# Second attention: the copy of the finished output groups moved from ScalarE to VectorE, at the head of the next step

## The chip, the core and the metric

The kernel runs on one core of a Trainium2 chip. The metric is the device time of one execution in microseconds (us). The engines are TensorE (PE in the rows; PEld is its weight load), ScalarE (ACT), VectorE (DVE), GpSimd (POOL) and SyncE (SP, which here only issues DMAs). Each engine works through its own instructions in order and waits for others on semaphores.

## The reference

Four layers follow one another on 16 sequences of 256 tokens with 128 features. Each is `x = x + layer(layernorm(x))`: a first attention with two heads, a feed-forward network, a second attention, and the same network again. The change lies in the second attention (16 heads of 8 features, causal):

```
qkv = encodings @ attn_w.T + attn_b
qkv = qkv.reshape(b, n, HEADS, 3 * HEAD).transpose(0, 2, 1, 3)
q, k, v = jnp.split(qkv, 3, axis=-1)
scores = jnp.einsum('bhki,bhqi->bhkq', k, q) / math.sqrt(HEAD)
scores = jnp.where(mask, scores, NEG_INF)
probs = jax.nn.softmax(scores, axis=2)
combined = jnp.einsum('bhkq,bhkl->bhql', probs, v)
out = combined.transpose(0, 2, 1, 3).reshape(b, n, HIDDEN)
return out @ out_w.T + out_b
```

## The kernel before, in words

The tokens are cut into 8 blocks of 512 (two sequences each), called 0 to 7 here. In the second attention a block takes 8 steps: 4 groups of 4 heads, times 2 sequences. Step `n` works on group `n // 2`, sequence `n % 2`. The loop is software-pipelined: while block `b` gets its exponentials and its output, block `b+1` gets its maxima, and block `b+2` its normalised input and its q and k.

On TensorE one step consists, in this order, of `pe_second` for the first head pair (the scores of block `b`, into two PSUM banks), `pe_first` (the scores of block `b+1`, from which only the row maxima are wanted; each has a last matmul with the mask), `pe_second` for the second pair, and `pe_values` of the step before (the probabilities times the values, into `o_bank`). Behind that, some steps carry one more piece: step 0 the transposes of the maxima, step 1 the transposes of the normalised input, steps 2 and 3 the q and the k product, step 4 the v product, step 5 more transposes of maxima, step 6 the output projection of block `b-1`.

ScalarE takes the exponential of each `pe_second` (`act_exp`, `b_prob`), copies the maxima (`act_max`, `b_negative_max`), the q and k products (`act_hi`) and the transposed input. GpSimd masks each exponential (`pool_mask`) and multiplies the output with the inverse denominators (`pool_normalise`). VectorE reduces each `pe_first` to maxima (`dve_first`, two instructions that write `b_segment_max`), and computes the layer norm: `bn_stats` and `bn_aggr` at the head of step 0, and `dve_apply` (`xn`) at the end of step 0. It also makes the low parts of q and k (`dve_lo`, heads of steps 3 and 4), adds the bias to v (`dve_v`, step 5) and adds the projected output to `X` (`dve_down`, step 7). The order on every engine is written out by hand in `pe_step`, `act_body`, `dve_body` and `pool_body`.

`o_bank` is one PSUM bank. It collects a group over two steps, is copied to `b_o`, and is free for the next group only then: the first `pe_values` of a group waits for `b_output_copied` (`s_oc`). When the fourth group of a block is copied, in the block that follows, SyncE stores `b_o` to DRAM (L1772), and when that has landed loads it back in another layout as `b_oT` (L1776) and its denominators as `b_den` (L1777). VectorE takes their reciprocal (`dve_inverse`, at the end of step 2), and SyncE stores and loads that too. The reciprocal stands in VectorE's queue ahead of the low part of q and of the maxima of step 3.

In block 7 no maxima remain to be made. TensorE, ScalarE and VectorE already work on the gate of the next network there: after steps 2, 4 and 6 TensorE makes a gate product, ScalarE its tanh, and VectorE four instructions on it (`f_gate`, `f_hidden`, `f_h_hi`, `f_h_lo`).

Of the kernel before, what the change touches and what calls it, by code (L numbers as in the profile page):

```python
# [26 lines left out]
SEQS = 2  # L27
# [16 lines left out]
GROUPS = 4  # L44
# [41 lines left out]
def build(nc, io):  # L86
    ctx = ExitStack()
    with ctx:
# [1102 lines left out]
        def attention_b(link):  # L1191
# [18 lines left out]
            o_sb = sb("b_o", [P, GROUPS, TOK])  # L1210
# [11 lines left out]
            o_bank = banks3[:, 2, :]  # L1222
# [259 lines left out]
            def act_out(act, b, g):  # L1482
                act.wait_ge(s_pv, STEPS * b.t + SEQS * (g + 1))
                if g == 0:
                    wait(act, s_os, 16 * b.t)
                nc.scalar.activation(o_sb[:, g, :], o_bank[:, :], ACT.Copy).then_inc(s_oc, 1)
# [13 lines left out]
            def act_body(act, b, before, one, two):  # L1500
                prev, nxt = link["prev"], link["next"]
                n1, n2 = b.after(1), b.after(2)
                for n in range(STEPS):
                    act_exp(act, b, n, 0)
                    if n == MAX1_AT + 1:
                        act_max_rows(act, b, 1)
                    if one and n == MAX0_AT + 1:
                        act_max_rows(act, n1, 0)
                    act_exp(act, b, n, 1)
                    if is_block(b, 0) and n == 0:  # L1510
                        prev["act_tail"](act)
                    if n and n % SEQS == 0:
                        act_out(act, b, n // SEQS - 1)
                    if before and n == 0:
                        act_out(act, b.after(-1), GROUPS - 1)
                    if n == MAX1_AT:
                        act_max(act, b, 1)
                    if two and n == T_AT:
                        act_xT(act, n2)
                    if two and n == Q_AT:  # L1520
                        act_hi(act, n2, 0)
                    if two and n == K_AT:
                        act_hi(act, n2, 1)
                    if one and n == MAX0_AT:
                        act_max(act, n1, 0)
                    if not one and n == T_AT:
                        act.wait_ge(s_pv, STEPS * LAST)
                        nxt["act_xhi"](act, FIRST_BLOCK)
                    if not one and n in GATE_AT:
                        nxt["act_tanh"](act, FIRST_BLOCK, GATE_AT[n], HEAD_PAIR)  # L1530
                if not one:
                    act_out(act, b, GROUPS - 1)
                    nxt["act_tanh"](act, FIRST_BLOCK, KC - 1, HEAD_PAIR)
                    nxt["act_xhi"](act, SECOND_BLOCK)
# [40 lines left out]
            def dve_max(dve, m, half):  # L1575
# [5 lines left out]
                nc.vector.tensor_tensor(mx[half][:, :, 1, :, :].rearrange("p s j g -> p g s j"),  # L1581
                                        part[:, :, :, :, 1], part[:, :, :, :, 2], ALU.max).then_inc(s_mx, 1)

            def dve_inverse(dve, b):

                dve.wait_ge(s_ol, 32 * (b.t + 1))
                nc.vector.reciprocal(den_inv[:, :], den[:, :]).then_inc(s_inv, 1)
# [6 lines left out]
            def dve_body(dve, b, before, one, two):  # L1594
# [3 lines left out]
                for n in range(STEPS):  # L1598
                    if two and n == 0:
                        norm.dve_stats(dve, n2)  # L1600
                    if two and n == Q_AT + 1:
                        dve_lo(dve, n2, 0)
                    if two and n == K_AT + 1:
                        dve_lo(dve, n2, 1)
                    if one and n == V_AT + 1:
                        dve_v(dve, n1)
                    if one and before and n == OUT_AT + 1:
                        dve_down(dve, b.after(-1))
                    if one:
                        dve_first(dve, n1, n)  # L1610
                    if is_block(b, 0) and n == 0:
                        prev["dve_down"](dve, LAST_BLOCK)
                    if two and n == T_AT - 1:
                        norm.dve_apply(dve, n2, False)
                    if one and n == MAX0_AT - 1:
                        dve_max(dve, n1, 0)
                    if one and not two and n == OUT_AT:
                        nxt["norm"].dve_stats(dve, FIRST_BLOCK)
                    if one and not two and n == STEPS - 1:
                        norm.dve_free(dve)  # L1620
                        nxt["norm"].dve_apply(dve, FIRST_BLOCK, True)
                    if not one and n == T_AT:
                        nxt["dve_xlo"](dve, FIRST_BLOCK)
                        nxt["norm"].dve_stats(dve, SECOND_BLOCK)
                    if not one and n in GATE_AT:
                        nxt["dve_gate"](dve, FIRST_BLOCK, GATE_AT[n], HEAD_PAIR)
                        nxt["dve_hlo"](dve, FIRST_BLOCK, GATE_AT[n])
                    if before and n == INVERSE_AT:
                        dve_inverse(dve, b.after(-1))
# [323 lines left out]
```

## Time and profile before

| | |
|---|---|
| median of 3 runs | 743.64 us (742.78 to 744.47) |
| the profiled execution | 742.03 us, span 740.2 us |
| busy: PE, DVE, ACT, POOL | 671.3, 493.8, 453.2, 431.1 us of the span |
| chain that ended last | PE 52%, DVE 15%, issue 10%, POOL 8%, ACT 8%, DMA 6% |
| copies of output groups on ScalarE | 32, first at 342.2 us, last at 553.3 us |

Times of rows count from the start of the span. The profiled execution, 742.03 us, stands 1.6 us under the median of the three runs. In a timeline row stand the start, the time from the start of the first of the grouped instructions to the end of the last, the engine, the line, the operation with output and inputs, the count, and in brackets how long the engine was idle before and what ended that.

### The profile page before, as it was taken

To read this page: it belongs to the slowest core of one execution; us is meant where nothing else is said; L and a number is where in the kernel's file an instruction comes from. 1 tells how busy PE (TensorE), PEld (TensorE's weight loads), DVE (VectorE), ACT (ScalarE), POOL (GpSimd) and SP (SyncE) were. 2 spreads that over 40 slices of the span, in tenths; PEclk is the share of its full clock that TensorE was granted. 3 is DMA by queue.
4 is the path that set the end of the run, shared out by engine and by line. 5 is a ranking of instruction groups with operands and counts; after the bars stand their busy time and mean duration, and the time that the engine had idled before them with its cause. 6 is when DMAs were issued, how large, how long until landed. Compare 5 with 4: busy or idle time off the path is not lost.

```text
span 740.2 us, 13952 instructions
## 1 busy us (share of the span) xinstructions
PE 671.3 (91%) x4706; PEld 470.9 (64%) x4706; DVE 493.8 (67%) x958; ACT 453.2 (61%) x801; POOL 431.1 (58%) x443
## 2 busy tenths in 40 slices
PE   3889997899999989998999999998788899999997
PEld 1455655577877766665555555555446677877785
DVE  6779997657765686466777777675658457766521
ACT  2678886465666655546666666665655465666664
POOL 4545552477787776443444554544555687787773
PEclk9999999899999999999999999999969999999999
DMA  6111320000000004432556565563112000000001
GB/s 188 39 26 35 62 30 2 0 1 0 1 0 0 1 1 138 148 115 76 201 183 205 193 206 184 190 206 103 63 35 84 0 15 14 0 14 15 15 14 29
DMA packets 33028, 52.47 MB, mean 71 GB/s; under 512 B 4560, under 2 KB 9680, under 8 KB 32976
## 3 DMA queue, kind: packets, MB, share of 16 engines
q1 hardware_dynamic: 32784, 51.53, 22.2%
q8 instruction: 30, 0.49, 0.3%
q10 hardware_dynamic: 192, 0.26, 0.1%
q14 instruction: 22, 0.18, 0.1%
HBM read 27.15 MB, written 24.38 MB: 70 GB/s over the span
## 4 chain that ended last, share of the span: by engine, by line
PE 52%; DVE 15%; issue 10%; POOL 8%; ACT 8%; DMA 6%; SPq 1%; DVEq 0%; ACTq 0%; POOLq 0%
PE banks L220 49%; ACT b_prob L1478 3%; DVE b_segment_max L1571 3%; DMA b_o_dram<-b_o 3%; POOL f_h_lo L1149 3%; POOL f_g_lo L1156 2%; DVE xn L182 2%; DVE a_mx L652 2%; ACT a_prob L553 1%; DMA b_den<-b_o_dram 1%; DVE a_prob L666 1%; PE banks L212 1%; ACT f_g_hi L1044 1%; POOL b_prob L1681 1%; DVE a_straight L637 1%
## 5 line engine op out<-in xcount | busy, mean ns | idle before, releaser
L1156 POOL TENSOR_TENSOR f_g_lo<-f_gelu,f_g_hi 128x512 fp32r<-128x512 f32 x127 | 167.2, 1325 | 62.4 <-ACT f_g_hi L1044 61.9
L1043 ACT ACTIVATE f_gelu<-banks,cols 128x512 f32<-128x512 f32 x128 | 88.4, 691 | 134.4 <-PE banks L220 111.6
L1681 POOL TENSOR_SCALAR_AFFINE_SELECT b_prob<-b_prob 128x512 f32<-128x512 f32 x128 | 82.2, 644 | 108.0 <-ACT b_prob L1478 107.7
L1571 DVE TENSOR_REDUCE b_segment_max<-banks 128x6 f32<-128x768 f32 x128 | 116.2, 949 | 34.2 <-PE banks L220 34.2
L1478 ACT ACTIVATE b_prob<-banks 128x768 f32<-128x768 f32 x128 | 102.4, 807 | 55.9 <-PE banks L220 55.9
L220 PE MATMUL banks<-f_g_hi,whi 128*128 128x512 f32 x320 | 130.3, 407 | 2.3 <-POOL f_g_lo L1156 1.8
L220 PE MATMUL banks<-f_g_lo,whi 128*128 128x512 f32 x320 | 126.6, 396 | 0.0
L1149 POOL TENSOR_TENSOR f_h_lo<-f_hidden,f_h_hi 128x512 fp32r<-128x512 f32 x60 | 77.5, 1292 | 58.6 <-DVE f_h_hi L1095 58.6
L220 PE MATMUL banks<-f_h_hi,whi 128*128 128x512 f32 x256 | 106.0, 414 | 3.9 <-POOL f_h_lo L1149 2.3
L220 PE MATMUL banks<-f_h_lo,whi 128*128 128x512 f32 x256 | 102.3, 400 | 0.0
L1044 ACT ACTIVATE f_g_hi<-banks,cols 128x512 fp32r<-128x512 f32 x128 | 87.5, 683 | 0.0
L1088 DVE SCALAR_TENSOR_TENSOR f_gate<-f_tanh,banks 128x512 f32<-128x512 f32 x64 | 43.4, 678 | 62.5 <-ACT f_tanh L1035 62.5
L220 PE MATMUL banks<-f_xn_split,whi 128*128 128x512 f32 x256 | 74.1, 414 | 0.7 <-DVE f_hidden L1092 0.6
L182 DVE TENSOR_SCALAR xn<-X,mv,rstd 128x128 f32<-128x128 f32 (+1 forms) x104 | 72.2, 760 | 0.5 <-POOL rstd L207 0.4
L220 PEld LDWEIGHTS banks<-f_g_hi,whi 128*128 128x128 f32 x320 | 60.3, 188 | 17.7 <-POOL f_g_lo L1156 3.6
L220 PEld LDWEIGHTS banks<-f_g_lo,whi 128*128 128x128 f32 x320 | 60.3, 188 | 13.1 <-issue 0.2
L220 PEld LDWEIGHTS banks<-f_h_hi,f_h_lo 32*128 32x128 f32 x512 | 37.2, 187 | 46.4 <-ACT b_prob L1478 23.5
L220 PE MATMUL banks<-f_h_hi,f_h_lo 32*128 32x256 f32 (+1 forms) x512 | 55.2, 304 | 10.9 <-ACT b_prob L1478 7.5
L220 PE MATMUL banks<-b_prob,b_values 128*16 128x256 f32 (+1 forms) x1024 | 57.2, 343 | 6.9 <-POOL b_prob L1681 5.5
L220 PEld LDWEIGHTS banks<-f_h_hi,whi 128*128 128x128 f32 x256 | 48.9, 191 | 22.1 <-ACT f_g_hi L1044 3.9
L220 PEld LDWEIGHTS banks<-f_xn_split,whi 128*128 128x128 f32 x256 | 49.7, 197 | 15.0 <-issue 1.8
L220 PEld LDWEIGHTS banks<-f_h_lo,whi 128*128 128x128 f32 x256 | 48.8, 191 | 11.4 <-issue 0.7
(125 smaller groups left out, 1051.4 us busy)
## 6 DMA issues: line engine op xcount, KB each, us to landing
f_h_hi<-b_q_dram SPq DMA_DIRECT2D x16, 512.0 KB, 4.2
f_h_lo<-b_k_dram SPq DMA_DIRECT2D x16, 512.0 KB, 5.1
b_o_dram<-b_o SPq DMA_DIRECT2D x8, 1024.0 KB, 4.3
b_q_dram<-b_q_hi SPq DMA_DIRECT2D x16, 256.0 KB, 3.4
b_k_dram<-b_k_hi SPq DMA_DIRECT2D x16, 256.0 KB, 3.7
w_stage<-in_wF SPq DMA_DIRECT2D x8, 352.0 KB, 3.4
b_q_dram<-b_q_lo SPq DMA_DIRECT2D x8, 256.0 KB, 3.5
b_k_dram<-b_k_lo SPq DMA_DIRECT2D x8, 256.0 KB, 3.5
```

The source lines that it names most:

```text
L182: nc.vector.tensor_scalar(xn[:, s, :], X[:, bass.ds(TILES * t + s, 1), :], mv[:, s, 0:1], rstd[:, s:s + 1], ALU.subtract, ALU.mult).then_i ...
L212: last = nc.tensor.transpose(bank[:, s * P:(s + 1) * P], xn[:, s, :], ident[:, :])
L220: return nc.tensor.matmul(out, lhsT, rhs, start=start, stop=stop)
L652: nc.vector.reduce_max(mx[s][:, :, :], score[:, :, :].rearrange("p h (q k) -> p h q k", q=2), AX.X).then_inc(s_mx, 1)
L1043: nc.scalar.activation(gf[c % 2][:, :], z_bank[c % 2], ACT.Gelu, scale=scale).then_inc(s_gf, 1)
L1044: nc.scalar.activation(hi[:, c, :], z_bank[c % 2], ACT.Gelu, scale=scale).then_inc(s_ghi[c % 2], 1)
L1088: nc.vector.scalar_tensor_tensor(out=uu[slot][:, :], in0=th[slot][:, :], scalar=1.0, in1=a[:, :], op0=ALU.add, op1=ALU.mult).then_inc(s_u, 1)
L1149: nc.gpsimd.tensor_tensor(hlo[n.odd][:, c, :], hf[c % 2][:, :], hhi[n.odd][:, c, :].bitcast(F32), ALU.subtract).then_inc(s_hlo[c % 2], 1)
L1156: nc.gpsimd.tensor_tensor(lo[:, c, :], gf[c % 2][:, :], hi[:, c, :].bitcast(F32), ALU.subtract).then_inc(s_glo[c % 2], 1)
L1478: nc.scalar.activation(prob[n % 2][:, p, :, :, :], second_banks(b, p)[:, :, 0:3 * P].rearrange("p b (c q) -> p c b q", c=3), ACT.Exp, scal ...
L1571: nc.vector.reduce_max(seg[:, g, s, 2 * p:2 * p + 2, :], first_pass[:, 2 * p:2 * p + 2, 0:3 * P].rearrange("p b (c k) -> p b c k", c=3), A ...
L1681: nc.gpsimd.affine_select(out=pr, in_=pr, compare_op=ALU.is_ge, fill=0.0, base=0, pattern=[[0, 4], [1, P]], channel_multiplier=-1).then_in ...
```

## The change

The function `dve_out` copies a finished group on VectorE. It is called ahead of the maxima (`dve_first`) in steps 3, 5 and 7 for groups 0, 1 and 2, and in step 1 of the next block for group 3. The calls of `act_out` in ScalarE's steps are gone; on ScalarE it stood behind the second exponential of steps 2, 4 and 6 and of step 0 of the next block. ScalarE keeps one copy: group 3 of block 7, behind its last step. `dve_out` waits for the same semaphores as `act_out` and counts the same one up.

```
--- before
+++ after
@@ act_body
                     act_exp(act, b, n, 1)
                     if is_block(b, 0) and n == 0:
                         prev["act_tail"](act)
-                    if n and n % SEQS == 0:
-                        act_out(act, b, n // SEQS - 1)
-                    if before and n == 0:
-                        act_out(act, b.after(-1), GROUPS - 1)
                     if n == MAX1_AT:
                         act_max(act, b, 1)
@@
+            def dve_out(dve, b, g):
+                dve.wait_ge(s_pv, STEPS * b.t + SEQS * (g + 1))
+                if g == 0:
+                    wait(dve, s_os, 16 * b.t)
+                nc.vector.tensor_copy(o_sb[:, g, :], o_bank[:, :]).then_inc(s_oc, 1)
+
@@ dve_body
                     if one and before and n == OUT_AT + 1:
                         dve_down(dve, b.after(-1))
+                    if before and n == 1:
+                        dve_out(dve, b.after(-1), GROUPS - 1)
+                    if n > 1 and n % SEQS:
+                        dve_out(dve, b, n // SEQS - 1)
                     if one:
                         dve_first(dve, n1, n)
```

VectorE's queue before, from the end of step 0 to the start of step 3 of a block in the middle (the reductions into `b_segment_max` are those of steps 0 to 3, in pairs):

```order
L1571 TENSOR_REDUCE b_segment_max<-banks 128x6
L182 TENSOR_SCALAR xn<-X,mv,rstd 128x128 [waits b_xn_transposed,b_ln_rstd]
L182 TENSOR_SCALAR xn<-X,mv,rstd 128x128 x3
L1571 TENSOR_REDUCE b_segment_max<-banks 128x6 [waits b_first_scores]
L1571 TENSOR_REDUCE b_segment_max<-banks 128x6
L1571 TENSOR_REDUCE b_segment_max<-banks 128x6 [waits b_first_scores]
L1571 TENSOR_REDUCE b_segment_max<-banks 128x6
L1587 RECIPROCAL b_den_inv<-b_den 128x64 [waits b_output_loaded]
L1557 SCALAR_TENSOR_TENSOR b_q_lo<-banks,cols,b_q_hi 128x512 [waits b_hi_ready]
L1571 TENSOR_REDUCE b_segment_max<-banks 128x6 [waits b_first_scores]
L1571 TENSOR_REDUCE b_segment_max<-banks 128x6
```

The same stretch of VectorE's queue after the change:

```order
L1567 TENSOR_REDUCE b_segment_max<-banks 128x6
L182 TENSOR_SCALAR xn<-X,mv,rstd 128x128 [waits b_xn_transposed,b_ln_rstd]
L182 TENSOR_SCALAR xn<-X,mv,rstd 128x128 x3
L1584 COPY b_o<-banks 128x512 [waits b_values_weighted]
L1567 TENSOR_REDUCE b_segment_max<-banks 128x6 [waits b_first_scores]
L1567 TENSOR_REDUCE b_segment_max<-banks 128x6
L1567 TENSOR_REDUCE b_segment_max<-banks 128x6 [waits b_first_scores]
L1567 TENSOR_REDUCE b_segment_max<-banks 128x6
L1589 RECIPROCAL b_den_inv<-b_den 128x64 [waits b_output_loaded]
L1553 SCALAR_TENSOR_TENSOR b_q_lo<-banks,cols,b_q_hi 128x512 [waits b_hi_ready]
L1584 COPY b_o<-banks 128x512 [waits b_output_stored,b_values_weighted]
L1567 TENSOR_REDUCE b_segment_max<-banks 128x6 [waits b_first_scores]
```

The first copy (group 3 of the block before) now stands behind the reduction and the `xn` of step 0; the second (group 0 of this block) behind the reciprocal and the low part of q.

VectorE's queue in block 7, at the end of the third gate's four instructions (`-` before, `+` after; `xn` and `X` belong to the input of the next network and to the output of block 6):

```order
 L1099 TENSOR_TENSOR f_h_lo<-f_hidden,f_h_hi 128x512 [waits f2_hidden_hi]
+L1584 COPY b_o<-banks 128x512 [waits b_values_weighted]
 L182 TENSOR_SCALAR xn<-X,mv,rstd 128x128 [waits f2_xn_transposed,f2_ln_rstd]
 L182 TENSOR_SCALAR xn<-X,mv,rstd 128x128 x3
-L1592 TENSOR_TENSOR X<-banks,X 128x512 [waits b_bias_added_to_x,b_projected]
+L1594 TENSOR_TENSOR X<-banks,X 128x512 [waits b_bias_added_to_x,b_projected]
```

Here the copy of group 2 stands behind the four instructions on the third gate; the copies of groups 0 and 1 stand in the same way behind the first gate and the reciprocal, and behind the second gate.

## Rows read from the trace of the kernel before

**Rows 1.** Waits, 335 to 555 us: who waited for whom, in total, times, longest
```profile
DVE b_den_inv L1587 <- DMA b_den<-b_o_dram: 10.7, 6, 2.6
```

**Rows 2.** Groups of instructions, 335 to 555 us: busy us, mean ns of one
```profile
L1486 ACT ACTIVATE b_o<-banks 128x512 f32<-128x512 f32 x32 | 19.1, 597 | 7.6 <-PE banks L220 5.6 <-DMA b_o_dram<-b_o 2.0
...
L1563 DVE TENSOR_TENSOR b_values<-banks,rows 128x512 f32<-128x512 f32 x7 | 4.8, 692 | 1.6 <-PE banks L220 0.8
L1557 DVE SCALAR_TENSOR_TENSOR b_k_lo<-banks,cols,b_k_hi 128x512 fp32r<-128x512 f32 x6 | 4.5, 751 | 4.3 <-ACT b_k_hi L1470 4.3
...
L1557 DVE SCALAR_TENSOR_TENSOR b_q_lo<-banks,cols,b_q_hi 128x512 fp32r<-128x512 f32 x6 | 4.0, 668 | 1.1 <-ACT b_q_hi L1470 1.1
...
L1095 DVE CAST f_h_hi<-f_hidden 128x512 fp32r<-128x512 f32 x3 | 1.3, 427 | 0.1
```

**Rows 3.** Chain of work that ended last, 440 to 470 us: start, us, what
```profile
444.15 0.83 DVE b_segment_max L1571
445.02 1.22 DVE xn L182 x4
...
446.66 1.82 DVE b_segment_max L1571 x2
448.48 0.04 issue
448.52 3.21 PE banks L220 x34
```

**Rows 4.** Timeline of block 4, end of step 0 to step 4, and step 7
```profile
444.08 0.60 ACT L1486 ACTIVATE b_o<-banks 128x512 f32<-128x512 f32 x1
...
444.58 0.59 ACT L1492 ACTIVATE b_negative_max<-banks 8x512 fp32r<-8x512 f32 x1
...
446.44 0.84 PE L220 MATMUL banks<-b_prob,b_values 128*16 128x256 f32 x16
...
451.75 0.69 ACT L1470 ACTIVATE b_q_hi<-banks,cols 128x512 fp32r<-128x512 f32 x1 [0.43 <-PE banks L220]
...
452.71 0.55 DVE L1587 RECIPROCAL b_den_inv<-b_den 128x64 f32<-128x64 f32 x1 [1.34 <-DMA b_den<-b_o_dram]
...
453.20 0.45 PE L220 MATMUL banks<-f_h_hi,f_h_lo 32*128 32x256 f32 x4 [0.34 <-ACT b_prob L1478]
...
453.58 0.84 PE L220 MATMUL banks<-b_prob,b_values 128*16 128x256 f32 x16
...
453.75 1.81 DVE L1571 TENSOR_REDUCE b_segment_max<-banks 128x6 f32<-128x768 f32 x2
...
455.62 0.39 PE L220 MATMUL banks<-f_h_lo,f_h_hi 32*128 32x256 f32 x2
...
467.23 1.82 DVE L1571 TENSOR_REDUCE b_segment_max<-banks 128x6 f32<-128x768 f32 x2 [0.33 <-PE banks L220]
```

**Rows 5.** Timeline of block 6, step 0 and step 4
```profile
497.98 1.82 DVE L1571 TENSOR_REDUCE b_segment_max<-banks 128x6 f32<-128x768 f32 x2 [0.69 <-PE banks L220]
...
499.16 0.60 ACT L1486 ACTIVATE b_o<-banks 128x512 f32<-128x512 f32 x1
...
510.46 0.65 PE L220 MATMUL banks<-f_h_lo,f_h_hi 32*128 32x256 f32 x8 [1.97 <-DVE b_segment_max L1571]
```

**Rows 6.** Timeline of block 7, `pe_values` of steps 2, 4 and 6 and VectorE beside it
```profile
535.57 0.84 PE L220 MATMUL banks<-b_prob,b_values 128*16 128x256 f32 x16 [1.40 <-ACT b_o L1486]
...
538.93 0.54 DVE L1587 RECIPROCAL b_den_inv<-b_den 128x64 f32<-128x64 f32 x1
...
542.57 1.48 PE L220 MATMUL banks<-b_prob,b_values 128*16 128x256 f32 x16
...
544.73 1.00 DVE L1099 TENSOR_TENSOR f_h_lo<-f_hidden,f_h_hi 128x512 fp32r<-128x512 f32 x1
...
551.74 1.48 PE L220 MATMUL banks<-b_prob,b_values 128*16 128x256 f32 x16 [2.08 <-POOL b_prob L1681]
```

**Rows 7.** Timeline: TensorE's first work after two other gaps
```profile
43.05 1.33 PE L449 MATMUL banks<-ident,a_prob 128*128 128x128 f32 x5 [2.74 <-ACT a_prob L568]
...
276.92 0.63 PE L212 MATMUL banks<-ident,xn 128*128 128x128 f32 x4 [2.26 <-DVE xn L182]
```

**Rows 8.** TensorE in three stretches: stretch, us, busy (count), granted clock, DMA share, GB/s
```profile
44.00:46.00 2.00, 2.00 (x7) 0.50 0.29 107
277.00:280.00 3.00, 3.00 (x16) 1.00 0.00 0
510.50:513.50 3.00, 3.00 (x28) 0.51 0.28 87
```

## Prediction

> **What bounds the kernel now.** I read the shares and the chain of the page first, then the waits of the stretch of the second attention (335 to 555 us), then the chain of waits and the timeline of one block in the middle, block 4, and last the two blocks that differ, 6 and 7. On the page TensorE is busy 91% and ends most of the chain; that would say that a copy on any other engine is free. The chain inside block 4 says otherwise [rows 3]: from the reduction of step 0 over `xn` to the reduction of step 1 it runs on VectorE, back to back, and TensorE's next first scores start 0.04 us after the reduction ends. So VectorE has no room just where two of the four copies will stand. The second thing to see is the wait for the denominators [rows 1]: six times VectorE stands until `b_den` has landed, 10.7 us in all. In block 4 it stands 1.34 us [rows 4]. Behind the reciprocal wait the low part of q and the reduction of step 3, which starts at 453.75 and, 1.81 us long, ends at 455.56; TensorE's first scores of step 4 start at 455.62. That wait is thus already at the edge of the path. Whatever makes the denominators later is paid by TensorE one for one.
>
> **What is taken away.** ScalarE loses 31 copies of 0.60 us [rows 2]. What does it gain on the path? In step 0 the copy of group 3 ends as `b_negative_max` starts (444.58), but that waits for TensorE's transposes, so it could start hardly earlier. In step 2 ScalarE stands idle for 0.43 us before `b_q_hi` until the q product is there, the copy being long over [rows 4]. Steps 4 and 6 have the v product and the output projection on TensorE in the same place. I value the removal at 0. The upper bound of the gain stands with the rivals.
>
> **What one copy costs on VectorE.** The trace has no VectorE copy from PSUM. Nearest are three-input and two-input passes over the same 128x512 from PSUM: 668, 692 and 751 ns; from below, the cast from SBUF at 427 ns [rows 2]. I take 0.66 us, by the nearest rows, and keep 0.43 and 0.75 as ends. Instructions that follow one another start about 0.08 us before the end of the one ahead: `b_den_inv` starts at 452.71, and after its 0.55 and the 0.67 of `b_q_lo` the reduction starts at 453.75 and not at 453.93, two overlaps in 1.04 us [rows 2, 4]. So a copy pushes what stands behind it by 0.58 and is itself complete after 0.66.
>
> The cast's 427 ns is a rate for data in SBUF. The Trainium skill (VectorE: DVE Perf Modes, "Why PSUM operands drop a tier") says that fp32 from PSUM gets no fast mode, and its table of cycles (same page, "The TRN2 errata") would give 120 + 512 cycles at 0.96 GHz, an estimate of 0.658 us. By it the lower end falls away; the sum is the same.
>
> **A block in the middle (1 to 5), step by step, on block 4's times.**
> - Step 7 of the block before: the copy of group 2 stands ahead of the reduction, before which VectorE was idle 0.33 us [rows 4]. It delays it by 0.58 - 0.33 = 0.25. The reduction, the maxima, statistics and `xn` behind it are back to back, so 0.25 arrives at step 1.
> - Step 1: the copy of group 3 starts where the reduction started, 446.66 + 0.25 = 446.91, and ends at 447.57. ScalarE had it done at 444.68. The output group is copied 2.9 us later. `pe_values` of step 0 (446.44) writes the same bank and must wait until 447.6: TensorE and all behind it, the transposes of the normalised input too, go back by 1.15 us.
> - The store, its landing, the load of the denominators: SyncE issues them one after another from the copy on, and nothing in them gets shorter. The reciprocal moves from 452.71 to 455.6.
> - Step 3: reciprocal and low part of q take 1.04, so the copy of group 0 starts at 456.65 and ends at 457.3. `pe_values` of step 2, which follows the second scores (453.20) and started at 453.58, now waits for that copy: 457.35, which is 3.75 later. The reduction starts at 457.23, ends at 459.05, and TensorE, with the k product still to do, reaches the first scores of step 4 at 455.62 + 3.75 = 459.4. The 1.15 of step 1 is contained in this 3.75, since the later wait swallows the earlier.
> - The copy of group 1 in step 5 stands behind the bias of v with some idle time around it: 0.2 at most, which the wait for the exponentials covers. Were that cover gone it would be 0.58.
> - SyncE's later queue (the q and k rows for block b+2) goes back with the block, not more: their deadlines shift by as much.
>
> Per block 3.75, five blocks: 18.8. Of this, copies of 0.43 us would take off three times 0.23, or 0.7 per block, and copies of 0.75 add 0.3.
>
> **Block 6.** No `xn` stands between. The reduction of step 0 starts at 497.98 [rows 5], plus 0.25, plus 1.82 less 0.08: the copy starts at 499.97 and ends at 500.63, where ScalarE's ended at 499.76. Denominators 0.9 later, the copy of group 0 adds 0.58, and the first scores of step 4, already waiting 1.97 for the reduction, come 1.5 later. Block 0 has three copies and no denominators: 0.3.
>
> **Block 7.** Nothing delays group 3, but groups 0 to 2 stand behind the gates. Step 3: the reciprocal at 538.93 is behind the first gate and cannot start much earlier, since the denominators are no sooner there; the copy follows at 539.4 and is done at 540.0. `pe_values`, at 535.57, comes 4.4 later. As ScalarE is free during that time, exponentials are ahead afterwards; I count 2.7 as staying. Step 5: `f_h_lo` ends at 545.73, the copy 0.58 later at 546.3, `pe_values` was at 542.57: 3.7. Step 7 is the same again, 4.0, less the 2.08 that TensorE waited for masks before the next `pe_values` [rows 6]: 1.9. Together 8.3.
>
> **The clock.** In the middle blocks TensorE will stand from the end of the second scores (453.20 + 0.45 + 1.15 = 454.8) to 457.35, a gap of 2.55 us. After the gap of 1.97 us that ended at 510.46 the granted clock was 0.51 (the 1.2 GHz level) for the 3 us from 510.5; after 2.74 us (43.05) it was 0.50; after 2.26 us (276.92) it stayed at 1.00 [rows 5, 7, 8]. In three microseconds at half clock TensorE, which is what bounds after the gap (values, k product, second scores), loses 1.5 us. I take the fall in every middle block: 5 x 1.5 = 7.5. Its bounds are 0 and, with one more low stretch per block, 15.
>
> The Trainium skill (TensorE: Matmul & The Clock Gate, "HAM oscillation — how this bites in real kernels") describes a loop with a wait in each turn that puts the clock back each time, at a price of half the throttled time. By that rule the fall recurs in every block; the row after 276.92 shows that a gap near this length need not do it.
>
> **The sum.** 18.8 + 1.5 + 0.3 + 8.3 = 28.9, with the clock 36.4. The profiled execution took 742.0, so 778.4; the median of the runs stood 1.6 higher: 780.
>
> **The rivals.**
> - The same waits, but the clock stays up: 743.6 + 28.9 = 772.5. For it speaks the one gap of 2.26 us without a fall, against it the other two.
> - The denominators' path is absorbed. If stores and loads run quicker once they are not beside the row loads, or if the first copy finds its place earlier, only the direct waits count: 1.15 in five blocks, and block 7: 5.8 + 0.3 + 8.3 = 14.4 on the median, 758, or somewhat less. Against it: the wait for `b_den` is in six of seven blocks already.
> - Not slower: ScalarE's exponentials are what holds TensorE in many steps (the second scores at 453.20 waited 0.34 for them), and with 31 copies gone the exponentials start earlier. If that pays 0.5 in each copy's step it is -15.5; if only where the negative maxima follow a copy, 7 x 0.5 = -3.5, and 740. It decides if VectorE's copies fall into its idle time, that is if step 1's reduction is not on the chain. The chain says it is [rows 3].
> - More than forecast: two low-clock stretches per block, or the late low part of q holds SyncE's queue so that the q and k rows come too late: 790 and above.
>
> **Chances.** Forecast 0.51 (own range 770 to 788), clock stays 0.24 (768 to 776), absorbed 0.13 (750 to 764), more 0.06, not slower 0.06, half of it within 0.2%. The range that holds eight in ten is 760 to 788. A measurement here tells about 0.2%, 1.5 us, from no change. Slower 0.94, same 0.03, faster 0.03.
>
> **What would show it.** In the profile after: `b_o` on VectorE near 0.66 us; in a middle block the copy of group 3 directly behind `xn`; `pe_values` of step 0 released by the copy with 1.1 us of wait; about 3 us of idle time before the reciprocal where it was 1.34, and `pe_values` of step 2 released by the copy of group 0 after 2.5 us; middle blocks 3.5 to 5.5 us longer each; a granted clock near 0.5 behind that gap in blocks 1 to 5. I am wrong if the middle blocks grow by less than 2 us, if the reciprocal does not move, or if ScalarE's exponentials release TensorE earlier in steps 2, 4 and 6.

## The result and the profile after

| | before | after |
|---|---|---|
| median | 744.06 us (742.78 to 749.5) | 785.07 us (783.79 to 787.98, 4 runs) |
| profiled execution | 742.03 us, span 740.2 us | 787.98 us, span 786.1 us |
| busy: PE, DVE, ACT, POOL | 671.3, 493.8, 453.2, 431.1 us | 689.4, 510.6, 436.3, 430.9 us |
| granted clock, mean | 0.976 | 0.944 |

The change made the kernel slower by 5.4% (ratio 1.0542, interval 1.0481 to 1.0603). Forecast were 780 us, so the forecast fell short by 5. Of the page after, lines of its parts 1, 2 and 4: busy time with share and instructions, the granted clock in 40 slices, the chain that ended last.

```profile
PE 689.4 (88%) x4706; PEld 479.5 (61%) x4706; DVE 510.6 (65%) x989; ACT 436.3 (56%) x770; POOL 430.9 (55%) x443
...
PEclk9999999999999999999898898998878989999999
...
PE 52%; DVE 19%; issue 9%; POOL 6%; DMA 6%; ACT 6%; DVEq 1%; SPq 0%; ACTq 0%; POOLq 0%
```

ScalarE is rid of 17 us and VectorE has 17 us more, neither of them near its limit. The span grew by 45.9. PE's busy time rose too, though it has no instruction more: the same matmuls at a lower clock.

The waits of the second attention after (335 to 602 us): in total, times, longest.

```profile
PE banks L220 <- DVE b_o L1584: 33.3, 13, 4.5
DVE b_den_inv L1589 <- DMA b_den<-b_o_dram: 22.0, 6, 4.7
```

The first line did not exist before; the second was 10.7 us for the same six waits [rows 1]. They are two ends of one thing: VectorE stands for the denominators, and TensorE stands for the copy that is queued behind them.

Block 4 after, timeline from the end of step 0 to step 4, VectorE, SyncE and the releases on TensorE:

```profile
468.97 1.69 DVE L182 TENSOR_SCALAR xn<-X,mv,rstd 128x128 f32 x4
470.58 0.68 DVE L1584 COPY b_o<-banks 128x512 f32<-128x512 f32 x1
...
471.29 0.36 SPq L1778 DMA_DIRECT2D b_o_dram<-b_o  x1
471.31 0.84 PE L220 MATMUL banks<-b_prob,b_values 128*16 128x256 f32 x16 [0.84 <-DVE b_o L1584]
...
477.88 0.44 PE L220 MATMUL banks<-f_h_hi,f_h_lo 32*128 32x256 f32 x4 [0.34 <-ACT b_prob L1478]
...
479.35 0.55 DVE L1589 RECIPROCAL b_den_inv<-b_den 128x64 f32<-128x64 f32 x1 [3.46 <-DMA b_den<-b_o_dram]
479.82 0.65 DVE L1553 SCALAR_TENSOR_TENSOR b_q_lo<-banks,cols,b_q_hi 128x512 fp32r<-128x512 f32 x1
480.39 0.68 DVE L1584 COPY b_o<-banks 128x512 f32<-128x512 f32 x1
...
481.13 1.48 PE L220 MATMUL banks<-b_prob,b_values 128*16 128x256 f32 x16 [2.81 <-DVE b_o L1584]
```

Read it downwards as one chain: `xn`, the copy of group 3 right behind it, SyncE's store 0.03 us after the copy's end, the reciprocal 8.1 us behind the store, the low part of q, the copy of group 0, and TensorE, which had stood 2.81 us. Against [rows 4] the reciprocal's idle time has grown from 1.34 to 3.46 us. The last row shows something else: the 16 matmuls take 1.48 us where they took 0.84. TensorE by stretches of the same block (us, busy and count, granted clock, DMA share, GB/s):

```profile
475.00:479.00 4.00, 2.98 (x34) 1.00 0.28 74
479.00:480.00 1.00, 0.00 (x0) 0.81 0.00 0
480.00:481.00 1.00, 0.00 (x0) 0.50 0.15 33
481.00:486.00 5.00, 4.87 (x33) 0.50 0.63 192
486.00:487.00 1.00, 1.00 (x11) 0.78 0.24 90
```

The clock fell to its lower level (1.2 GHz) while TensorE stood, at about 479.6, and came back at about 486.4. In blocks 1 to 5 it fell each time in this gap, which was 3.61, 3.21, 2.51, 2.81 and 2.86 us long; in block 6 it fell 0.5 us after TensorE had resumed. The same view of blocks 1 to 5 after, one row each, and of all five before:

```profile
363.10:397.50 34.40, 27.32 (x324) 0.90 0.47 159
397.50:430.80 33.30, 27.68 (x324) 0.90 0.49 161
430.80:465.80 35.00, 29.66 (x324) 0.85 0.47 152
465.80:498.80 33.00, 27.80 (x320) 0.90 0.49 163
498.80:530.90 32.10, 27.03 (x322) 0.95 0.51 168
```

```profile
359.80:496.80 137.00, 126.83 (x1600) 1.00 0.59 196
```

**Where the 45.9 us of span are.** I measure a block from the first copy into `b_max` at its head to the next block's. The heads of blocks 1, 6 and 7, before, then after:

```profile
359.75 0.18 DVE L1579 COPY b_max<-b_segment_max 128x16 f32<-128x16 f32 x1
...
496.84 0.37 DVE L1579 COPY b_max<-b_segment_max 128x16 f32<-128x16 f32 x1
...
527.47 0.17 DVE L1579 COPY b_max<-b_segment_max 128x16 f32<-128x16 f32 x1
```

```profile
363.11 0.18 DVE L1575 COPY b_max<-b_segment_max 128x16 f32<-128x16 f32 x1
...
530.88 0.31 DVE L1575 COPY b_max<-b_segment_max 128x16 f32<-128x16 f32 x1
...
564.25 0.16 DVE L1575 COPY b_max<-b_segment_max 128x16 f32<-128x16 f32 x1
```

Blocks 1 to 5 took 137.1 us and take 167.8: +30.7. Block 6 took 30.6 and takes 33.4: +2.7. Ahead of block 1 there are 3.4 us. Block 0's head comes 1.4 later, behind code that the change doesn't touch: the clock fell at 278.2 behind a gap of 2.27 us, and behind the same gap it had stayed up before [rows 7, 8]. In block 0 a stretch at the lower clock, 332.8 to 336.3, costs about 1.6, as its matmuls of 128x512 take 0.63 us and not 0.40. The execution of the profile was also the slowest of the four, 2.9 us over their median. Block 7, from its head to the second `pe_values` of step 7, took 24.3 us and takes 33.0: +8.7. Its rows:

```profile
574.80 0.54 DVE L1589 RECIPROCAL b_den_inv<-b_den 128x64 f32<-128x64 f32 x1
575.26 0.62 DVE L1584 COPY b_o<-banks 128x512 f32<-128x512 f32 x1
576.03 1.48 PE L220 MATMUL banks<-b_prob,b_values 128*16 128x256 f32 x16 [4.50 <-DVE b_o L1584]
...
586.03 1.48 PE L220 MATMUL banks<-b_prob,b_values 128*16 128x256 f32 x16 [3.87 <-DVE b_o L1584]
...
596.03 2.76 PE L220 MATMUL banks<-b_prob,b_values 128*16 128x256 f32 x32 [3.84 <-DVE b_o L1584]
```

From block 7's head these three are at 11.8, 21.8 and 31.8 us; they were at 8.1, 15.1 [rows 6] and 21.4. The second half of the last row, from 597.26, is what stood at 551.74. TensorE also had its lower clock for about 18.6 us of this stretch where before it had it for 10.2; what that costs beside the waits is not separated here. The sum, 30.7 + 2.7 + 3.4 + 8.7, is 45.5; the other 0.4 of the 45.9 lie behind block 7's last `pe_values`.

### The profile page after: what moved, and what is told of

It reads as the page before. It is cut to its first block, busy times and chain, and to the rows that moved or that the text cites. A ratio compares the mean times of both kernels' runs of the same rounds, so it can differ in the third digit from the quotient of the medians.

```text
span 786.1 us, 13950 instructions
## 1 busy us (share of the span) xinstructions
PE 689.4 (88%) x4706; PEld 479.5 (61%) x4706; DVE 510.6 (65%) x989; ACT 436.3 (56%) x770; POOL 430.9 (55%) x443
## 4 chain that ended last, share of the span: by engine, by line
PE 52%; DVE 19%; issue 9%; POOL 6%; DMA 6%; ACT 6%; DVEq 1%; SPq 0%; ACTq 0%; POOLq 0%
PE banks L220 49%; DMA b_o_dram<-b_o 4%; DVE b_segment_max L1567 3%; DVE xn L182 3%; POOL f_h_lo L1149 2%; DMA b_den<-b_o_dram 2%; ACT b_prob L1478 2%; POOL f_g_lo L1156 2%; DVE a_mx L652 2%; DVE b_o L1584 2%; ACT a_prob L553 1%; DVE f_hidden L1092 1%; PE banks L212 1%; DVE a_prob L666 1%; DVE stats L171 1%
## 5 line engine op out<-in xcount | busy, mean ns | idle before, releaser
L220 PE MATMUL banks<-b_prob,b_values 128*16 128x256 f32 (+1 forms) x1024 | 62.9, 371 | 36.0 <-DVE b_o L1584 33.3
L220 PE MATMUL banks<-f_xn_split,whi 128*128 128x512 f32 x256 | 75.7, 421 | 1.3 <-DVE f_hidden L1092 1.0
L220 PEld LDWEIGHTS banks<-f_g_lo,whi 128*128 128x128 f32 x320 | 60.9, 190 | 13.4 <-issue 0.2
L220 PE MATMUL banks<-f_h_hi,f_h_lo 32*128 32x256 f32 (+1 forms) x512 | 56.4, 318 | 10.4 <-ACT b_prob L1478 7.6
L220 PEld LDWEIGHTS banks<-b_prob,b_values 128*16 128x16 f32 x1024 | 25.8, 103 | 59.0 <-issue 27.4
```

The source lines that it names most:

```text
L220: return nc.tensor.matmul(out, lhsT, rhs, start=start, stop=stop)
```

## The experiments

The theory: the time goes to the place of the copies, not to their engine. Group 3's copy behind `xn` makes the denominators late, and that holds the copy of group 0 and with it TensorE; block 7 pays apart; the clock falls behind the gaps. Rivals: the copies' own time on VectorE, ScalarE's share in the path, or the clock as the real cause.

### Group 3 back on ScalarE

```
+ if before and n == 0: act_out(act, b.after(-1), GROUPS - 1)   # in act_body
- if before and n == 1: dve_out(dve, b.after(-1), GROUPS - 1)   # in dve_body
```

> The changed kernel, with the copy of group 3 (block b-1) given back to ScalarE in step 0; groups 0 to 2 stay on VectorE. Theory (position: the time is lost because the copy of group 3 stands behind the reduction and xn of step 0, which makes the denominators and with them step 3 late): the denominators come as before, a middle block keeps only the copy of group 0 behind the low part of q, 0.8 us, no gap of TensorE over 2 us and so no fall of the clock there; block 7 keeps its 8 to 9 us. Sum 5 x 0.8 + 0.8 + 0.4 + 8.9 = 14, about 758 us. Rival (load: VectorE simply has 31 copies of 0.6 us more to do, wherever they stand): seven copies fewer of 31 give back a fourth to a fifth of the 41 us, about 776 us.

Measured: 763.09 us (759.73 to 764.39), ratio 1.0251 (1.0186 to 1.0317): without this one copy 22 us of the 41 are gone, 5 fewer than expected. `b_den_inv` waits 9.4 us in all, where it was 10.7 before the change. Block 3:

```profile
430.04 0.55 DVE L1591 RECIPROCAL b_den_inv<-b_den 128x64 f32<-128x64 f32 x1 [1.22 <-DMA b_den<-b_o_dram]
431.08 0.68 DVE L1586 COPY b_o<-banks 128x512 f32<-128x512 f32 x1
...
431.82 0.84 PE L220 MATMUL banks<-b_prob,b_values 128*16 128x256 f32 x16 [0.64 <-DVE b_o L1586]
```

With the denominators on time the copy of group 0 still stands between the low part of q and the reduction. TensorE waits 0.64 us for it, and a middle block is 0.9 to 1.0 longer than before where the clock stays up (1.3 in block 5), where 0.8 was expected. So the miss of 5 us lies elsewhere: in the profiled execution the clock fell in block 2 all the same (1.8 us more than its neighbours), block 6 is 2.3 longer and not 0.8, and block 0's head comes 0.8 later, behind a fall of the clock in code that no run changed.

### Group 3 alone on VectorE

```
+ if n and n % SEQS == 0: act_out(act, b, n // SEQS - 1)        # in act_body
- if n > 1 and n % SEQS: dve_out(dve, b, n // SEQS - 1)         # in dve_body
```

> The other half: only the copy of group 3 is on VectorE (head of step 1), groups 0 to 2 are back on ScalarE. Position theory: the denominators come 2.65 us later in blocks 1 to 5, the first scores of step 4 with them; TensorE's gap splits around pe_values of step 2 and stays near 1 us, so the clock falls rarely; block 6 0.7, block 7 nothing: +14, about 758 us, up to 768 if the clock falls in each block. Load rival: 7 copies of 31, a fourth to a fifth of 41 us: about 753 us.

Measured: 761.12 us (759.5 to 765.36), ratio 1.0235 (1.0162 to 1.0308). One copy out of four costs 17 us by itself; VectorE waits 21.3 us for the denominators, much as after the full change (22.0), while TensorE waits only 3.5 us for `b_o`. Blocks 2 and 4, in which the clock stayed up, are 2.4 and 2.2 us longer (29.7 and 29.5 against 27.3), block 5 is 1.2. So in e1 0.9 and here 2.3, together 3.2 of the 4.0 that a block with all copies takes (section "Work for TensorE in the gap"). The rest appears only when both are there, that is when the copy of group 0 itself stands behind the late reciprocal; for the runs, 19.4 for groups 0 to 2 and 17.4 for group 3 make 36.8 of the 41. In blocks 1 and 3 the clock fell here too, against the expectation that it would do so rarely.

### Block 7's copies back on ScalarE

```
+ if not one and n and n % SEQS == 0: act_out(act, b, n // SEQS - 1)
- if n > 1 and n % SEQS: dve_out(dve, b, n // SEQS - 1)
+ if one and n > 1 and n % SEQS: dve_out(dve, b, n // SEQS - 1)
```

> The changed kernel with only block 7's groups 0 to 2 back on ScalarE (three copies). Position theory: the copies behind the gates cost 8.9 us in the profile (block 7 from 527.47 to the last values against 564.25 to there), so 785 - 9 = 776 us. Load rival: 3 of 31 copies, 785 - 4 = 781 us.

Measured: 776.35 us (772.84 to 778.69), ratio 1.0408 (1.0336 to 1.0479), 8.7 us under the change as a whole, which is what the trace of the change says for block 7. Three copies in the last block cost half as much as group 3's copy alone does in all blocks (17.4).

### All copies on VectorE, but early

```
+ if before and n == 0: dve_out(dve, b.after(-1), GROUPS - 1)   # behind the reduction of step 0,
+ if n and n % SEQS == 0: dve_out(dve, b, n // SEQS - 1)        # and of steps 2, 4, 6
```

Here all 31 copies stand behind the reduction of the even step, ahead of `xn`, of the reciprocal and of the gates.

> All 31 copies on VectorE as in the changed kernel, but each one place earlier: directly behind the reduction of the even step in which ScalarE made them (group 3 behind the reduction of step 0, ahead of xn; groups 0 to 2 behind the reductions of steps 2, 4, 6, group 0 thus ahead of the reciprocal; in block 7 ahead of the gates). Position theory: group 3 is done at 445.7 instead of 444.7 in block 4, the denominators 1.0 us later, 1.0 to 1.2 per block over 6 blocks, block 7 1 to 2: about 752 us and no clock falls in blocks 1 to 4. Load rival: the same 31 copies cost the same, about 780 us.

Measured: 747.56 us (745.38 to 753.02, 10 runs), ratio 1.0053 (1.0021 to 1.0085). The same engine with the same copies (682 ns each) costs 3.8 us instead of 41. The waits of the stretch, as above:

```profile
DVE b_den_inv L1589 <- DMA b_den<-b_o_dram: 9.6, 6, 2.4
...
PE banks L220 <- DVE b_o L1584: 0.6, 1, 0.6
```

This is the run that decides: the engine is nearly free, the place is not. In its trace blocks 1 to 5 take 141.0 us, where it was 137.1 before and 167.8 after the change, with the clock at its upper level throughout. Block 6 takes 33.1 (30.6 before), with two stretches at the lower clock, and from block 7's head to the end it is 3.0 us shorter than before, where TensorE had waited 1.40 us for ScalarE's copy [rows 6] and then had its lower clock for 10.2 us.

### Early, and group 3 on ScalarE

The version that the runs so far point to: groups 0 to 2 early on VectorE, group 3 on ScalarE in step 0.

```
+ if before and n == 0: act_out(act, b.after(-1), GROUPS - 1)   # in act_body
+ if n and n % SEQS == 0: dve_out(dve, b, n // SEQS - 1)        # behind the reduction of steps 2, 4, 6
```

> Groups 0 to 2 on VectorE, directly behind the reduction of steps 2, 4 and 6 (group 0 thus in the idle time ahead of the reciprocal), group 3 on ScalarE in step 0 as before. Position theory: group 0 falls into 1.3 us of idle time, group 2 into 0.9 us, group 1 delays the maxima by up to 0.5, of which 0.1 to 0.2 reaches TensorE; the denominators come as before; in block 7 ScalarE no longer stands behind the store of the block before. 742 to 745 us, the same as before. Load rival: 24 of 31 copies at VectorE's price, 744 + 24 x 0.6 = 758 us.

Measured: 744.27 us (740.9 to 745.7, 12 runs), ratio 0.9993 (0.9961 to 1.0025): no loss and no gain that can be told from the noise. Blocks 1 to 5 take 137.7 us against 137.1 before. This way did not beat the kernel before, and the next run shows how little there was to gain.

### What ScalarE's copies are worth

```
- nc.scalar.activation(o_sb[:, g, :], o_bank[:, :], ACT.Copy)
+ nc.scalar.activation(o_sb[:, g, 0:8], o_bank[:, 0:8], ACT.Copy)
```

This is the kernel before, with 8 of 512 columns copied. It leaves out the rest of the attention's output (`b_o` is filled once on GpSimd). A copy takes 178 ns in place of 597, so 13.4 of ScalarE's 19.1 us are taken away.

> The kernel before with ScalarE's 32 copies cut to 8 of 512 columns in the same places (rest of b_o filled once on GpSimd during the network before; the output is not the reference's). It measures what freeing ScalarE is worth. Theory (worth nothing): 743 to 744 us, at most 1 us less in block 7. Rival (the exponentials start earlier where a copy stood): -3.5 us if only step 1's, -15 if each.

Measured: 742.32 us (738.47 to 746.27, 12 runs), ratio 0.9984 (0.9959 to 1.0008). Freeing ScalarE of seven tenths of that time is worth about 1 us; the interval reaches from a gain of 3 us to a loss of 0.6. The "not slower" rival, with its gains of 3.5 to 15.5 us, had little to stand on: against the 28.9 us of new waits it would have needed a gain as large.

### Tiny copies on VectorE

The same cut of the copy in the kernel after, in the places of the change.

> The changed kernel with VectorE's copies cut to 8 of 512 columns, in the same places and with the same waits; the rest of b_o is filled once on GpSimd during the network before (so the output is not the reference's). Position theory: a place costs also without a copy. In block 4 group 3 is released at 446.8 instead of 444.7, denominators 2.1 later, pe_values of step 2 2.4 later, TensorE's gap 2.1 us; block 7's copies still stand behind the gates, 7.5. Sum 5 x 2.4 + 0.7 + 7.5 = 20, and 0 to 10 of clock: 764 to 774 us. Rival (VectorE's time for the copies): back to 746.

Measured: 780.08 us (772.89 to 794.44), ratio 1.043 (1.0382 to 1.0478), above the expected 764 to 774. The run of 794.44 had a mean granted clock of 0.829, the others 0.943 to 0.958; without it the median is 778.8. Group 3's copy and the copy of group 0 in block 3:

```profile
435.75 0.15 DVE L1586 COPY b_o<-banks 128x8 f32<-128x8 f32 x1
...
443.96 0.55 DVE L1591 RECIPROCAL b_den_inv<-b_den 128x64 f32<-128x64 f32 x1 [3.41 <-DMA b_den<-b_o_dram]
445.00 0.16 DVE L1586 COPY b_o<-banks 128x8 f32<-128x8 f32 x1
...
445.21 1.48 PE L220 MATMUL banks<-b_prob,b_values 128*16 128x256 f32 x16 [1.99 <-DVE b_o L1586]
```

A copy that takes 0.15 us in place of 0.68 has the reciprocal wait 3.41 us, as the full one did (3.42 in this block), and TensorE 1.99 us. From the head the reciprocal is 2.2 and `pe_values` of step 2 is 2.6 later than in block 4 before, where 2.1 and 2.4 were expected. Taking the copies' duration away gives back 5 of 41 us by the medians, 6 without the run of 794.44, 8 by the ratios; standing behind the wrong instruction is the rest. What I had counted too low is the clock: in gaps of 2.0 to 2.7 us it fell in every middle block, and in the profiled execution it was at its lower level for 44 us of blocks 1 to 5, where it was for 34 in that of the full copies. Those five blocks took 167.4 and 167.8 us. So what the duration alone is worth in a middle block stays hidden behind the clock.

### The reciprocal one step later

```
- INVERSE_AT = 2
+ INVERSE_AT = 3
```

In the kernel after, this moves the reciprocal behind the low part of q, the copy of group 0 and the reduction of step 3.

> The changed kernel with the reciprocal one step later on VectorE (end of step 3 in place of step 2), so that the wait for the denominators stands ahead of neither the low part of q, nor the copy of group 0, nor the reduction of step 3. Theory (the denominators' wait is what carries the delay of group 3's copy to TensorE): of 3.75 us per middle block about 1.2 stay, no clock falls there, but SyncE sends the q and k rows of block b+2 behind the inverse, up to 2 us of that may come back as a wait for rows; block 7 as before: 763 to 771 us. Rival (the copies' own time is what counts, the denominators are hidden): unchanged, 785.

Measured: 769.74 us (767.59 to 780.84), ratio 1.0336 (1.0299 to 1.0373), 15 us below the change. The run of 780.84 had a mean granted clock of 0.94, the others 0.96 to 0.966. But it brought a new wait, `f_h_lo` from the stored k rows, 11.5 us in five waits, since SyncE stores those rows behind the inverse denominators. So the same edit was run in the kernel before:

> The kernel before with the reciprocal one step later (end of step 3). Does the wait for the denominators cost it something already? It stood in blocks 5 and 6 (27.76 us, and 30.63 with a gap of 1.97 and a fall of the clock); both would lose it, -0.5 and -3. Against that SyncE sends the q and k rows of block b+2 some 2.7 us later; their loads landed about 0.4 us before use, so about 2 us per block in blocks 1 to 5 would be a wait for rows. If the rows bind: 750 us; if they do not: 740 us.

Measured: 761.15 us (752.78 to 762.5), ratio 1.0194 (1.011 to 1.0278), 11 us above the higher of the two answers: the rows bind, and cost more than I had counted. Its waits:

```profile
PE banks L220 <- DMA f_h_lo<-b_k_dram: 11.6, 5, 3.6
```

The row wait comes from the place of the reciprocal alone; without it that line was 0.3 us, once. On this base the copies on VectorE cost only 769.7 - 761.2 = 8.6 us (by the ratios 10.6), about block 7's 8.7. In the traces blocks 1 to 5 take 152.5 and 151.8 us; but the clock was at its lower level for 14 us of them with the copies on VectorE and for 24 us without. With the denominators' wait out of the way of group 0's copy, little of the middle blocks' loss is left beside a row wait that could cover some of it; how much it covers these two runs do not say.

### Work for TensorE in the gap

Two tries at the clock. First 12 matmuls of the scores' shape, thrown away, behind the second scores of step 3; then three projections of 128x512.

```
+ if one and before and n == 3: pe_filler(pe, b, n)             # ahead of pe_values
```

> The changed kernel with work for TensorE in its long gap: in step 3 of blocks 1 to 6, ahead of pe_values of step 2, twelve matmuls of the second scores' shape (32 rows, 128 or 256 columns; three times 0.45 us) into the two score banks once their last exponential is taken; nothing reads them. They end at about 480.6 in a block where pe_values waited until 481.13, so they delay nothing, and the gap of 2.8 us becomes 0.9 and 0.6. Clock theory (the falls after the gap are a term of their own, about 12 us over blocks 1 to 5): the granted clock stays at 1.00 there and 785 becomes 773 to 776. Rival (what TensorE does at half clock lies beside other waits, or the clock falls all the same): 783 to 786.

Measured: 785.17 us (782.56 to 789.36), ratio 1.0575 (1.0534 to 1.0615): the rival's answer. The 12 matmuls took 0.91 us at the upper clock and left up to 1.5 us open behind them, and the clock fell in blocks 2 to 6. In four of these five blocks it fell before the open rest came: in block 2 at 407.89, the filler having started at 407.85, and in blocks 3, 5 and 6 within 0.6 us of the filler's start. Ahead of that stood only the two short pauses that each block has before the filler, in block 2 of 0.33 and 0.90 us. It stayed up in block 1, which gives one clean figure (363.49 to 394.82, TensorE's row of that stretch):

```profile
363.50:394.80 31.30, 26.25 (x332) 1.00 0.52 174
```

A middle block with all copies and no fall takes 31.3 us, 4.0 more than before. It is the only one of its kind.

> The changed kernel with heavier work in TensorE's gap of step 3 in blocks 1 to 6: three projections (128 rows, 512 columns, 0.56 us each) into the score banks once their last exponential is taken; nothing reads them. The lighter work of the experiment before filled 0.9 us and the clock fell all the same in four of five blocks; the one block in which it stayed up took 31.3 us where those with falls took 32.3 to 33.5. If the clock stays up with this: 5 blocks of 31.4 instead of 33.6 us, 785 - 11 = 774 us. If it falls all the same or the work itself runs past the copy (three at half clock take 3.3 us), 785 or more.

Measured: 783.38 us (781.52 to 784.39), ratio 1.0515 (1.044 to 1.0589). Timeline of block 1, TensorE's rows in step 3 and VectorE's copy, and TensorE by stretches:

```profile
374.41 0.45 PE L220 MATMUL banks<-f_h_hi,f_h_lo 32*128 32x256 f32 x4 [0.73 <-ACT b_prob L1485]
375.76 4.54 PE L220 MATMUL banks<-xnT,wB 128*128 128x512 f32 x6 [0.90 <-ACT b_prob L1485]
...
377.95 0.68 DVE L1591 COPY b_o<-banks 128x512 f32<-128x512 f32 x1
...
380.23 0.84 PE L220 MATMUL banks<-b_prob,b_values 128*16 128x256 f32 x16
```

```profile
373.00:376.00 3.00, 1.37 (x13) 1.00 0.39 99
376.00:379.50 3.50, 3.50 (x5) 0.51 0.06 11
379.50:382.00 2.50, 2.50 (x20) 1.00 0.62 178
```

The condition of the second answer came, its time nearly (785 or more): the gap was filled and the clock fell all the same, in five of six blocks (1 to 6), here at 376.0, after pauses of no more than 0.73 and 0.90 us. It came back sooner, and the mean clock is 0.965 instead of 0.944. But the filler ran mostly at half clock itself (4.54 us) and ended 1.6 us behind the copy. It was also sized too large: with the clock up, in block 4, the three projections take 2.84 us, 0.95 each and not 0.56, and end 1.2 behind the copy. So it bought back little, and this way the price of the clock can't be isolated.

## Why the prediction was right

The step times are given from the block's head, so that they can be laid beside [rows 4] (head at 441.78; after at 465.80).

- **Removal worth nothing.** Holds as far as it was measured: 0.8 us by the medians (742.3 against 743.1 of the kernel before beside it) for seven tenths of the copies' time, with an interval that reaches to 3 us.
- **One copy 0.66 us, push 0.58.** 0.68 us, and the next instruction starts 0.60 behind its start. The Trainium skill (VectorE: DVE Perf Modes, "The TRN2 errata") gave an estimate of 0.658 us; the rows agree within 0.02.
- **Group 3 copied 2.9 later.** From the head 2.90 before, 5.46 after, 2.56; the 0.25 of step 7 lies before the head, so 2.8. Of the 0.25 the rows show 0.2: the reduction of step 7 starts 1.21 us behind the start of the addition to `X`, and 1.02 before.
- **`pe_values` of step 0 waits 1.15.** It waited 0.84; the head itself came a little later.
- **Reciprocal 2.9 later, `pe_values` of step 2 3.75 later.** From the head 2.6 and 3.5, with the 0.25 again 2.9 and 3.8. Gap 2.55 forecast, 2.81 measured, and 3.0 on average over blocks 1 to 5. The one block with all copies and no clock fall is 4.0 longer.
- **Blocks 6, 0 and 7.** Block 7: 8.7 against 8.3, with the first two waits together 6.7 at `pe_values` of step 4, where 6.4 was forecast, and all three 10.4 at that of step 6, as forecast. Block 0 outside its clock stretch: 0.4 against 0.3. Block 6: 2.7 against 1.5. The reciprocal came 0.55 later, less than the 0.9 forecast, but TensorE stood 2.86 us for the copy, and the clock, low from 510.6 to 514.0 before, is now low from 544.5 to 551.3: the forecast counted the fall for the middle blocks only, and in block 6 the stretch at the lower clock has doubled.
- **The clock, 7.5.** This term of the sum was mis-sized. Blocks 1 to 5 grew 30.7; five times 4.0 is 20.0, so 10.7 fall to the clock, 2.1 per block and not 1.5. (The 4.0 rests on one block, so this division is an estimate.) The 1.5 took three microseconds at half clock as the whole; in block 4 it was low from 479.6 to 486.4, of which the first 1.5 us are the gap itself.
Set against the forecast's 36.4: 20.0 + 10.7 + 2.7 + 0.4 + 8.7 = 42.5. The rest of the 45.9 is 3.0 of chance clock ahead of block 1 and 0.4 behind block 7. The terms came out 6.1 above their forecast: 3.2 the clock in the middle blocks, 1.2 their waits, 1.2 block 6, 0.4 block 7, 0.1 block 0. All five terms were too small, so the forecast is not near by errors that cancelled. By the medians the change is 41.0, 4.6 above the forecast's 36.4; the profiled execution was the slowest of its four, and shows more than they do.

Of the rivals, "clock stays up" (772.5) is out, since the granted clock fell in every block of the profiled execution; "absorbed" (758) is out, since the reciprocal moved by the whole delay; "not slower" is out by the kernel before with tiny copies; "more" (790) was nearer than I held it, as block 3 with its mean clock of 0.85 shows, the worst of the five.

**What stays open:** what decides whether the clock falls. With the filler the pauses ahead of it were 0.34 and 0.90 us in block 4 and 0.33 and 0.91 in block 5; in block 4 the clock stayed, in block 5 it fell. And the gap of 2.26 us ahead of 276.9, in code that no run changed, shows both outcomes (last section). So the number of falls in one execution is partly chance, and of the 10.7 us one can say what they were, not that the next execution has them in the same blocks.

## What to carry to other kernels

An engine that is 65% busy is not free at a given place. Before moving a copy, write down what stands ahead of it in the new queue and what that waits for; here a DMA wait stood ahead, and the bank's next writer inherited it. Put a copy that frees a bank or starts a store as early as its input allows, ahead of anything that waits for a DMA, and ahead of long chains: the same copies, placed so, cost 3.8 us and not 41. And test the gain first: eight columns instead of 512 on the old engine show in one run about what freeing it can bring; here that left 0.18 us of each 0.60 us copy in place.

## What the runs showed of the hardware that was not expected

The wait of the first network that ends near 276.9, the same in every kernel here, is an experiment that nobody had to make. TensorE stands 2.25 to 2.49 us for `xn`. Its granted clock in the six microseconds behind it, first in the kernel of "all early", then in that of "group 3 back on ScalarE":

```profile
277.00:283.00 6.00, 6.00 (x27) 1.00 0.00 0
```

```profile
277.00:283.00 6.00, 6.00 (x22) 0.80 0.00 0
```

Of the 13 profiled executions, 7 have the clock at its lower level in the microseconds that follow and 6 have it at 1.00, after the same work and nearly the same gap (both values occur with 2.26 us). A gap of this length went either way here, so the forecast's "fall in every middle block" was not safe from the two rows behind which it fell; why the middle blocks fell each time was not settled. Not even a filled gap is safe: in the run with three projections TensorE worked without a pause from 375.76 on, and its clock was lowered at 376.0.

Two things more. The kernel before with tiny copies has one block, block 2, that takes 30.3 us instead of 27.3. Its rows:

```profile
401.25 0.55 DVE L1588 RECIPROCAL b_den_inv<-b_den 128x64 f32<-128x64 f32 x1 [3.58 <-DMA b_den<-b_o_dram]
402.43 1.94 PE L220 MATMUL banks<-xnT,wB 128*128 128x512 f32 x2 [1.72 <-DVE b_q_lo L1558]
```

The copy of group 3 was not late. SyncE issued the load of `b_oT` 5.6 us behind the store, where it was 4.3 in the same block of the kernel before, and the reciprocal started 4.5 us behind the issue of the denominators' load, where it was 2.9. So VectorE waited 3.58 us for the denominators and not 1.81, TensorE stood 1.72 us for the low part of q, and the clock was low from 402.6 to 406.0. So the path that the change lengthens can cost time without the change too, where its DMAs come late: 3.0 us in this one block, half of what a middle block lost by the change in its profile (6.1). A trace of one execution has to be cleared of such blocks before stages are compared. And the medians hide a spread: without the run of 794.44, three runs with tiny copies on VectorE still lie between 772.9 and 781.4 us, so that a difference of a few us between kernels with many falls, each with four runs, says little.
